# First part of a Haar-convolution block: the right neighbour of every fourth chunk moves from PE to DVE, the statistics of y1 from DVE to ACT

## What is computed

```python
def layer0(x):                      # x1 = x + layer0(groupnorm(x))
    s = bilinear_shift(x, theta_s)  # each channel shifted by less than one pixel in y and x
    return einsum('bchw,oc->bohw', s * w_dw, w_pw)

def layer1(x1):                     # x1 + layer1(groupnorm(x1))
    h = concat(haar_dwt(x1))        # 4 bands of 128 x 128
    h = gelu(batchnorm(conv1x1(h, w_c1, b_c1)))   # y1 is the output of this conv1x1
    o = layernorm(dwconv3x3(h)); o = conv1x1(gelu(conv1x1(o))) + h
    return haar_idwt(gelu(batchnorm(conv1x1(o, w_c2, b_c2))))
```

## Time and profile before

| | |
|---|---|
| median of 3 runs | 5567.97 us (5566.92 to 5568.93) |
| the profiled execution | 5569.18 us, its span 5567.3 us |
| mean granted TensorE clock | 0.949 |
| PE busy | 4574.4 us, 82% |
| DVE busy | 4818.3 us, 87% |
| ACT busy | 4172.1 us, 75% |
| GpSimd (POOL) busy | 1108.8 us, 20% |
| moved by DMA | 1610.74 MB, 289 GB/s over the span |

### The profile page before, as it was taken

One profiled execution on the slowest core, in us unless ns is written; L12 is line 12 of the kernel. 1 busy time (PEld: TensorE's weight loads), 2 busy tenths in 40 slices (PEclk: granted clock), 3 DMA queues, 4 the chain that ended last, 5 costly groups with the idle time before them and its releaser, 6 DMA issues.

```text
span 5567.3 us, 54045 instructions
## 1 busy us (share of the span) xinstructions
PE 4574.4 (82%) x12292; PEld 2104.5 (38%) x12292; DVE 4818.3 (87%) x4463; ACT 4172.1 (75%) x5706; POOL 1108.8 (20%) x779
## 2 busy tenths in 40 slices
PE   1889999999999999999961777777897777777775
PEld 0334444444444444444420444444553222222222
DVE  6999898988989889899739999999939888888887
ACT  4887777777777777777635777777749888888887
POOL 0000000000000000000028777777601111111111
PEclk6999999999999999999985999999999999999998
DMA  8999999999999999999972333333219999999999
GB/s 338 370 360 409 426 425 425 415 426 426 417 426 416 426 425 417 423 370 392 355 257 72 118 117 117 117 119 121 99 25 216 237 235 236 236 236 235 237 235 224
DMA packets 256299, 1610.74 MB, mean 289 GB/s; under 512 B 30256, under 2 KB 30640, under 8 KB 92336
## 3 DMA queue, kind: packets, MB, share of 16 engines
q1 hardware_dynamic: 164016, 1005.35, 45.5%
q0 software_dynamic: 36864, 268.45, 23.2%
q10 hardware_dynamic: 55296, 335.57, 14.4%
HBM read 946.55 MB, written 662.70 MB: 289 GB/s over the span
## 4 chain that ended last, share of the span: by engine, by line
PE 35%; DMA 23%; DVE 16%; POOL 12%; issue 7%; ACT 3%; DVEq 0%; POOLq 0%; ACTq 0%; SPq 0%
DMA out_x<-arena 18%; PE ps L753 13%; PE ps L741 11%; PE ps L736 10%; POOL arena L427 5%; POOL arena L432 5%; DMA arena<-in_x 4%; DVE arena L1249 2%; DVE arena L1112 2%; POOL arena L413 2%; ACT arena L698 2%; DVE arena L1098 2%; DVE arena L1362 2%; DVE arena L1127 1%; DVE ps L1238 1%
## 5 line engine op out<-in xcount | busy, mean ns | idle before, releaser
L909 PE MATMUL ps<-arena,c2T 128*128 128x512 f32 x2048 | 1023.3, 651 | 367.4 <-ACT arena L691 365.1
L741 PE MATMUL ps<-arena 128*128 128x512 f32 x2048 | 965.1, 595 | 24.9 <-DVE arena L1127 24.9
L753 PE MATMUL ps<-arena 128*128 128x512 f32 x2048 | 963.8, 614 | 15.8 <-DVE small L1076 13.8
L736 PE MATMUL ps<-arena 128*128 128x512 f32 x1920 | 913.2, 598 | 43.2 <-DVE arena L1047 22.8
L413 POOL TENSOR_SCALAR arena<-arena,taps 128x1024 f32<-128x1024 f32 (+1 forms) x256 | 285.6, 1116 | 2918.5 <-ACT arena L609 2887.1
L489 ACT ACTIVATE arena<-ps,small 128x1024 f32<-128x1024 f32 x512 | 568.0, 1109 | 321.6 <-PE ps L741 321.0
L1238 DVE SCALAR_TENSOR_TENSOR ps<-arena,taps,ps 128x1024 f32<-128x1024 f32 (+1 forms) x640 | 784.0, 1282 | 6.7 <-ACT ps L635 6.0
L691 ACT ACTIVATE arena<-ps,small 128x512 f32<-128x512 f32 x1024 | 713.7, 778 | 97.8 <-DVE arena L1354 89.8
L1098 DVE SCALAR_TENSOR_TENSOR arena<-arena,shift 128x2048 f32<-128x2048 f32 x256 | 601.6, 2350 | 200.9 <-DMA arena<-in_x 150.9
L909 PEld LDWEIGHTS ps<-arena,c2T 128*128 128x128 f32 x2048 | 401.4, 205 | 988.6 <-ACT arena L691 559.7
L467 ACT ACTIVATE ps<-arena 128x1024 f32<-128x1024 f32 x512 | 526.4, 1028 | 169.8 <-ACT arena L489 159.6
(11 more groups left out here) (164 smaller groups left out, 5249.0 us busy)
## 6 DMA issues: line engine op xcount, KB each, us to landing
arena<-in_x SPq DMA_DIRECT2D x400, 1024.0 KB, 16.1
out_x<-arena ACTq DMA_DIRECT2D x256, 1024.0 KB, 9.1
arena<-out_x SPq DMA_DIRECT2D x256, 1024.0 KB, 17.0
out_x<-arena POOLq DMA_DIRECT2D x256, 1024.0 KB, 17.0
arena<-in_x SPq DMA_DIRECT2D x112, 1152.0 KB, 15.5
y_dram<-arena ACTq DMA_DIRECT2D x128, 512.0 KB, 8.6
arena<-y_dram SPq DMA_DIRECT2D x128, 512.0 KB, 3.3
h_dram<-arena SPq DMA_DIRECT2D x112, 512.0 KB, 2.6
```

What stands on the lines that cost most here:

```text
L736: mm(ps[:, r, :], w_right[:, :], u_buf[k][:, 2 * r:2 * r + 2, 2:W + 2], start=False, stop=False, skip_group_check=True)
L741: last = mm(ps[:, r, :], w_center[:, :], v_buf[k][:, r * BANK:(r + 1) * BANK], start=False, stop=True, skip_group_check=True)
L753: last = mm(ps[:, 4 + s % 2, :], w_c1b[:, q, :], cells[:, q // 2, q % 2, :, :], start=(q == 0), stop=(q == 3))
L909: last = mm(ps[:, 4 * k + q, :], c2T[:, q, :], h2[:, k * HC:(k + 1) * HC], start=True, stop=True)
```

## The change

In images 0 to 6 the chunks of slot 3, one in four, now have the right neighbour added on DVE, as the odd chunks of image 7 have had, and PE leaves their two pairs of right-neighbour matmuls out. In such a chunk the third count of x ahead moves from before v's first addition to between its two. `count_y1` and its aggregates go from DVE. ACT's eviction of y1 gets a sum, and a new `square_y1` on ACT squares 128 x 512 elements with a sum, after `sum_x` of the same chunk. At the end one reduction over 256 sums takes the place of the aggregates.

```diff
-        stats_y1 = cut(B * NCH * 6)
-        mom_y1 = cut(2 * B).rearrange("p (a b) -> p a b", a=2)
+        sums_y1 = cut(2 * B * NCH).rearrange("p (a n) -> p a n", a=2)
+        y1_squares = cut(BANK // 2).bitcast(BF16)
...
         def three_in_v(b, s):
 
-            return final(b) and s % 2 == 1
+            return s % 2 == 1 if final(b) else s == SLOTS - 1
...
                 nc.scalar.activation(y1_out[k][:, half * HC:(half + 1) * HC], ps[:, 4 + half, :],
-                                     ACT.Identity, bias=bias1).then_inc(y1_ready, 1)
+                                     ACT.Identity, bias=bias1,
+                                     accum_out=sums_y1[:, 0, bass.ds(c, 1)]).then_inc(y1_ready, 1)
...
+            def square_y1(b, g, s):
+                c = b * NCH + g * SLOTS + s
+                act.wait_ge(y1_ready, nth(c))
+
+                act.wait_ge(y1_counted, nth(c, 1))
+                nc.scalar.activation(y1_squares, y1_out[s // 2][:, (s % 2) * HC:(s % 2 + 1) * HC], ACT.Square,
+                                     accum_out=sums_y1[:, 1, bass.ds(c, 1)]).then_inc(y1_counted, 1)
...
                         sum_x(*ahead_of, s)
+                    if chunk:
+                        square_y1(*chunk)
                     take_x1(b, g, s, 0, first)
...
-            def count_y1(b, g, s):
-                c = b * NCH + g * SLOTS + s
-                dve.wait_ge(y1_ready, nth(c))
-                nc.vector.bn_stats(stats_y1[:, bass.ds(c * 6, 6)],
-                                   y1_out[s // 2][:, (s % 2) * HC:(s % 2 + 1) * HC]).then_inc(y1_counted, 1)
...
-                if ahead_of and not late:
+                if ahead_of and not late and not three_in_v(b, s):
                     count_x(*ahead_of, s, range(2, DVE_PIECES))
-                if before and not three_in_v(b, s):
-                    if not first:
-                        count_y1(b - 1, g - 1, s)
-                    elif tail:
-                        count_y1(b - 2, NG - 1, s)
                 dve.wait_ge(u_done, nth(t))
                 v = v_buf[k].rearrange("p (r c) -> p r c", c=W)
                 left_added = stt(out=v, in0=u_buf[k][:, :, 0:W], scalar=left, in1=u, op0=ALU.mult, op1=ALU.add)
                 if three_in_v(b, s):
                     left_added.then_inc(v_left, 1)
-                    if before:
-                        count_y1(b - 1, g - 1, s) if not first else count_y1(b - 2, NG - 1, s)
-                    dve.wait_ge(v_left, g * 2 + (s // 2 + 1))
+                    if ahead_of and not late:
+                        count_x(*ahead_of, s, range(2, DVE_PIECES))
+                    dve.wait_ge(v_left, g * 2 + ((B - 1) * NG + s // 2 + 1) if final(b) else b * NG + (g + 1))
                     stt(out=v, in0=u_buf[k][:, :, 2:W + 2], scalar=right, in1=v,
                         op0=ALU.mult, op1=ALU.add).then_inc(v_done, 1)
...
+            dve.wait_ge(y1_ready, nth(B * NCH, 1))
             dve.wait_ge(y1_counted, nth(B * NCH, 1))
-            aggregate_y1(B - 1)
-            done(nc.vector.tensor_reduce(part[:, :], mom_y1, mybir.AxisListType.X, ALU.add))
-            done(ts(mom, part[:, :], 1.0 / B, None, ALU.mult))
+            done(nc.vector.tensor_reduce(part[:, :], sums_y1[:, :, :], mybir.AxisListType.X, ALU.add))
+            done(ts(mom, part[:, :], 1.0 / (B * HH * HW), None, ALU.mult))
```

More of the change, by code:

```diff
@@ L451, in _ @@
                 act.sem_inc(stored, 16)
-            for counter in (x_summed, x_in_psum, x1_ready, sq_done, y1_ready, h_ready, dw_put,
+            for counter in (x_summed, x_in_psum, x1_ready, sq_done, y1_ready, y1_counted, h_ready, dw_put,
                             a_ready, hT_ready, o_squared, g_ready):
@@ L537, in shift_group @@
                 for s in range(SLOTS):
+                    chunk = None
                     if before:
                         if s == SLOTS - 1:
-                            make_y1(b - 1, g, 0)
+                            chunk = (b - 1, g, 0)
                         elif not first:
-                            make_y1(b - 1, g - 1, s + 1)
+                            chunk = (b - 1, g - 1, s + 1)
                         elif tail:
-                            make_y1(b - 2, NG - 1, s + 1)
+                            chunk = (b - 2, NG - 1, s + 1)
+                    if chunk:
+                        make_y1(*chunk)
                     if first and s == 1 and before:
@@ L585, in _ @@
                 make_y1(B - 2, NG - 1, s)
+                square_y1(B - 2, NG - 1, s)
             square_root(2 * B)
@@ L590, in _ @@
                     make_y1(B - 1, g, s)
+                    square_y1(B - 1, g, s)
             square_root(2 * B + 1)
@@ L923, in _ @@
             stt, ts, tt = nc.vector.scalar_tensor_tensor, nc.vector.tensor_scalar, nc.vector.tensor_tensor
-            for counter in (x_counted, u_done, y1_counted, h2_ready, s_done):
+            for counter in (x_counted, u_done, h2_ready, s_done):
                 dve.sem_inc(counter, LEAD)
@@ L1179, in _ @@
             image(B - 1, before=True, tail=True, following=False, beyond=False)
[L1180 to L1185, removed]
             x1_moments(B - 1)
-            for s in range(SLOTS):
-                count_y1(B - 2, NG - 1, s)
             group_variance(2 * B, gmom, ps_small)
```

## The result

The kernel after takes 5583.64 us, the median of 9 runs (5580.53 to 5586.36); the kernel before takes 5568.10 us beside it (9 runs, 5565.93 to 5571.48). The ratio is 1.0028 with an interval of 1.0018 to 1.0037: slower by 15.5 us, a little more than what a measurement can tell from no change. The forecast was 5577 us, its range 5562 to 5594. The profiled execution took 5584.93 us, and its span is 5583.2 us, against 5569.2 and 5567.3 before.

What follows compares the result with a forecast made beforehand. It took DMA to bound images 1 to 6, DVE image 0, and PE and DVE both image 7. Terms +21.6 - 6 - 6 - 0.5 gave +9 us, so 5577 us, range 5562 to 5594.

Steps and rivals of the forecast that it cites:

- Image 0 and the first group of image 1 (+21.6): Nine groups where DVE has no count of y1 to lose: 2.4 us more each, +21.6 us, bounds 20 and 26.
- The matmuls in images 1 to 6 (0): PE falls from 41.9 to 38.4 us a group, but DMA stays at 42.5, so nothing is gained inside these images.
- The rival in which DMA looks full but would follow: Images 1 to 6: the removed matmuls count and ACT's 41.5 us sets the group, -60 us, 5517 us; chance 0.10.
- The sign that was to speak for it, a window of 100 us above 430 GB/s: Any such window in images 1 to 6 would show that the 426 GB/s taken as DMA's wall is not one.
- The rule of the Trainium skill that points the same way: DMA ceiling of 435 GB/s: images 1 to 6 would shrink by 2%, some 41 us, to about 5536 us; not adopted.
- Five image ends (-6): DMA's gap at image ends: a ring load comes 1.2 us earlier at each of five, -6 us, bounds 0 and -18.6.
- Image 6 to 7 (-6): Start of image 7: 4.5 us of DVE's wait for PE plus 2.0 from counts, taken as -6, bounds -2 and -7.
- ACT (0): New square and sums add 0.6 to 1.0 us a chunk; ACT needs 41.5 us a group, under 42.5: nothing, cover thin.
- The rival in which ACT becomes the bound: Chunk 3 of each group: ACT falls behind, its copies into PSUM come late, +14 and +6 us, 5597 us; chance 0.12.
- The end of the part (-0.5): End of part one: a square and one sum replace the last count and aggregate, -0.5 us, bounds -1 and +1.
- the rival in which nothing is given back (5590): Image ends and image 7's pads give no time back; only DVE's 21.6 us remain, 5590 us; chance 0.18.
- PE was to be 8% less busy in images 1 to 6: Sign of being right: images 2 to 5 at 340 to 343 us, DMA at 1.01, PE some 8% less busy.

Runs made afterwards that it cites:

- skip_start: Kernel after, with the right neighbour left on PE in image 0 and the first group of image 1: 5563.15 us, ratio 0.9991 to the kernel before.
- right_only: Kernel before, with only the right neighbour moved to DVE in every fourth chunk; DVE keeps the statistics of y1: 5588.91 us, ratio 1.0039.
- three_squares: Kernel after, with two more squares of y1 per chunk on ACT whose result nobody reads: 5664.04 us, ratio 1.0168 to the kernel before.
- stats_only: Kernel before, with only the statistics of y1 moved from DVE to ACT; the matmuls stay on PE: 5568.57 us, ratio 0.9999.
- skip_ends: Kernel after, right neighbour left on PE in image 0 and the first and last group of images 1 to 6: 5564.65 us, ratio 0.9992 to before.
- two_squares: Kernel after, with one more square of y1 per chunk on ACT whose result nobody reads: 5593.00 us, ratio 1.0040 to the kernel before.
- left_on_pe: Kernel after without the change in image 0 and image 1's first group; PE adds the left neighbour in image 0's fourth chunks: 5565.75 us, ratio 0.9995.
- after_half: Kernel after, with each load of x1 moving half its bytes: 5463.14 us, ratio 0.9811 to the kernel before.

## Why the prediction was right, and where its sum was off

**Image 0 and the first group of image 1 (+21.6).** The price was right, 2.4 us a group and +19.4 at the start of image 1. That DVE pays there and nobody gives anything back was shown by skip_start. But the ninth of these groups should not have been counted. The first group of image 1 did get 2.9 us longer (38.6 to 41.5), and the next two made up for it (42.3 and 41.9 before, 39.4 and 39.9 after), as in right_only. Over the whole of image 1 only 0.9 us were left.

**The matmuls in images 1 to 6 (0).** Right, and the term that mattered most: 8% of PE's matmuls went there, and images 2 to 6 moved by 1.1 of 1707.8 us. Half the x1 bytes turned the same matmuls into 77 us. The rival in which DMA looks full but would follow is excluded by the two kernels taken together. The sign that was to speak for it, a window of 100 us above 430 GB/s, is in none: the highest of the kernel after shows 426. The rule of the Trainium skill that points the same way (DMA: Bandwidth & Descriptors, Specifications, a ceiling of 435 GB/s) is not borne out by these traces as a rate that this mix of loads and stores reaches: 421 or 422 over 1980 us of images 1 to 6 stayed in the kernel before, in the kernel after, and in the six experiments with whole loads other than three_squares.

**Five image ends (-6).** This is the step that failed: "Over all, 422 instead of 426 GB/s for 1980 us is 18.6 us lost, 3.7 at each of five ends." The earlier load that I described did happen. The ring load of the last group's third chunk was issued 14.9 us before the next image's start in the kernel before (1757.02 to 1771.95), and 16.1 us in the kernel after:

```profile
1774.89 0.33 SPq L302 DMA_DIRECT2D arena<-in_x  x1
```

That is the 1.2 us forecast. What failed is the price per end, the number of ends, and above all the step from a smaller gap to a shorter kernel. The windows of the 70 us around an image start (52 before its first addition, 18 behind), in the kernel before into images 2, 4 and 5, then in the kernel after into images 4 and 5:

```profile
690.57:760.57 70.00, 70.00 (x166) 30.57 (x166) 66.03 (x79) 54.52 (x90) 0.00 (x0) 1.00 1.01 425
1377.33:1447.33 70.00, 66.58 (x156) 28.41 (x155) 65.75 (x79) 50.73 (x81) 0.00 (x0) 1.00 0.99 409
1719.95:1789.95 70.00, 66.59 (x156) 28.41 (x156) 66.10 (x79) 50.52 (x81) 0.00 (x0) 1.00 0.99 410
...
1397.06:1467.06 70.00, 62.98 (x143) 26.61 (x142) 66.70 (x74) 55.00 (x102) 0.00 (x0) 0.98 1.01 417
1739.01:1809.01 70.00, 62.13 (x134) 25.94 (x133) 67.93 (x74) 53.58 (x98) 0.00 (x0) 0.93 1.00 409
```

There is no gap at the end of image 1 (425 GB/s), so there are four and not five. Each of the four falls short of 426 GB/s by 2.7 to 3.3 us in the kernel before, not 3.7. In the kernel after, three of them are smaller by 1.3 to 1.6 us, and that of image 4 is as large as it was (410 and 409 GB/s). But the stretches between the ends, some 273 us each, lost what the ends had won. "Short" is the time less the bytes moved at 426 GB/s (from the view of DMA over each stretch), summed over images 2 to 5:

| kernel | short at the 4 ends, us | short in the 4 stretches between, us | mean image, us |
|---|---|---|---|
| before | 11.6 | 2.4 | 342.95 |
| after | 7.4 | 5.4 | 342.8 |
| stats_only | 7.1 | 6.5 | 343.1 |
| right_only | 7.0 | 7.1 | 342.9 |
| skip_start | 8.6 | 5.2 | 342.9 |
| skip_ends | 6.2 | 6.7 | 342.7 |

So the change won 4.2 us at the ends, near the forecast's 1.2 for each, lost 3.0 between them, and images 2 to 5 together are 0.5 us shorter. The step's error was to count what is won at an end as won for the kernel. Its reason for the gain is not the whole of it either: right_only keeps both counts ahead of that load, and its ends are as short. Why the stretches between move 1 to 2 GB/s less whenever the ends move more stays open; no run took that apart.

**Image 6 to 7 (-6).** Right in kind, too large: -3.7. The first group went from 40.5 to 36.1 us, by 4.4, which lies in the forecast's own "4.5 + 2.0" and "-2 and -7"; the second became 0.7 us longer (36.3 to 37.05). The reason for the second shows in PE's timeline: the first c1 behind the wait for its weights, in the kernel after and then in skip_start, whose instructions here are the same:

```profile
2505.83 5.48 PE L769 MATMUL ps<-arena 128*128 128x512 f32 x8 [2.55 <-DVE small L1086]
...
2484.13 3.87 PE L771 MATMUL ps<-arena 128*128 128x512 f32 x8 [2.14 <-DVE small L1088]
```

The same eight records took 1.6 us more. The granted clock, 1.00 at 2500 to 2506 us, was 0.60 and 0.55 in the next two windows of 2 us, so in part at the lower of its two levels, 1.2 GHz, after 2.55 us in which PE had no work:

```profile
2506.00:2508.00 2.00, 2.00 (x3) 0.76 (x4) 2.00 (x1) 1.89 (x2) 0.00 (x0) 0.60 1.03 432
```

The second group takes 35.45 us in skip_start, and the two groups are worth -5.3 us there against the kernel before, close to the forecast. In two_squares and left_on_pe the clock fell at this place as in the kernel after (37.05 us); in three_squares it did not, behind the same 2.55 us of idle time (35.45 us). So 1.6 of the 2.3 us that this term was short are the clock, and whether it falls here differs from execution to execution. The two causes were told apart: the first group takes 39.1 us with the statistics alone (-1.4), and likewise in skip_ends, where the matmuls of the last group are back; the remaining 3.0 us come with the matmuls (2.5 in right_only).

**ACT (0).** Right, and on the cautious side. The timeline of ACT shows what it gained:

```profile
1610.43 0.61 ACT L540 ACTIVATE arena<-arena 128x512 bf16<-128x512 f32 x1
1610.95 0.19 ACT L540 ACTIVATION_READ_ACCUMULATOR arena<-arena  x1
1611.05 1.10 ACT L489 ACTIVATE arena<-ps,small 128x1024 f32<-128x1024 f32 x1
```

From its start to the next instruction the square with its read takes 0.62 us: the read lies almost wholly beside other work, where I had added two reads to the 0.62 and came to at most 1.0. The chunk costs ACT 9.9 us (after_half, three_squares), not 10.4. The rival in which ACT becomes the bound was real but further off than its price: it needed one more square in image 7 and two more in the middle.

**The end of the part (-0.5).** +0.7, within its bounds of -1 and +1: the last eviction, the square and its read stand in a row on ACT, and DVE's sum waits for them.

**Together.** The forecast's form was right (DVE pays in image 0, DMA hides the rest, a little comes back) and landed 6.6 us low, because two terms of -6 were worth -1.1 and -3.7. The form held for the reasons that it gave; of the two terms, the first failed by its step, the second mostly by the clock. The result lies between the forecast and the rival in which nothing is given back (5590). One of the signs to look for was too large: PE was to be 8% less busy in images 1 to 6 and is 5% less (1954 to 1851 us), with 8% fewer matmuls. Its granted clock is 0.98 instead of 1.00, and the c1 matmuls take 641 ns instead of 614 in images 3 and 4. Images 2 to 6 are no longer for it, as PE does not set the pace there; at the start of image 7 it cost the 1.6 us above.

## What to carry to other kernels

Before taking work off an engine without idle time, ask what would be next: multiply out the bytes of a period, divide by the rate over a whole period, and compare; if the landings get later while the engine stays full, the engine is living on a lead, not setting the pace. Take the rate of whole periods as the wall, not that of the best stretch, and count time won or lost at a period's end only if the groups between the ends can't even it out. Price an edit in each stage separately: the stage without the compensating half (image 0 here, where DVE had no statistics to give away) paid for all of it.

## What the runs showed that was not expected

- Six kernels (before, after, stats_only, right_only, skip_start, skip_ends) with different work on DVE, ACT and PE have mean times of images 2 to 5 between 342.7 and 343.1 us, while single groups inside them moved by 2 to 3 us.
- The share of the DMA engines does not say what they move: 0.98 at 378 GB/s with PE as the bound, 1.03 at 383 in a stretch of 10 us, 1.01 at 422 over images.
- A square of 128x512 on ACT, listed at 0.61 us, added 0.52 us to a chunk where ACT was the bound, and its accumulator read of 0.19 us added 0.1.
- The same eight c1 matmul records at the start of image 7 took 3.87 or 5.48 us behind 2 to 3 us without work on PE, with the granted clock at 1.00 or near 0.6; kernels with the same instructions there show either.
- What the DMA queues moved more at the image ends they moved less between them, in all five kernels compared with the one before.
- The granted clock in image 0 fell from 0.98 (186 to 404 us of the kernel before) to 0.92 (205 to 423 us) when PE lost a sixth of its matmuls there, 401 to 332 in the windows.
